# Routing and gathering of layer-one expert inputs as side steps of the context attention loop

## The reference

```python
x = x + _L1_xattn_ref(_layernorm(x), ctx_1024, ...)   # 8 heads of 64
x = x + _L1_ffn_ref(_layernorm(x), ...)
# _L1_ffn_ref, for each sequence:
logits = x @ router_w + router_b                      # 112 x 8
top_k_logits, expert_indices = jax.lax.top_k(logits, 2)
expert_probs = jax.nn.softmax(top_k_logits)
pos = cumsum(one_hot(first choices, then second)) ... - 1   # rank of a row within its expert
expert_inputs = buf.at[ei, pos].add(xr)               # 8 x 33 x 256, rows beyond 33 are dropped
# then silu((einp @ w_c_fc + b) * (einp @ w_gate + b)) @ w_c_proj + b, and each row collects its two outputs
```

## Time and profile before

| | |
|---|---|
| median of 3 runs | 1946.5 us (1944.9 to 1956.9) |
| profiled execution | 1952.7 us, its span 1951.1 us |
| mean granted TensorE clock | 0.946 |
| PE busy | 1719.9 us (88% of the span) |
| DVE busy | 1177.2 us (60%) |
| ACT busy | 828.2 us (42%) |
| POOL busy | 452.9 us (23%) |

### The profile page before, as it was taken

One profiled execution on the slowest core, in us unless ns is written; L12 is line 12 of the kernel. 1 busy time (PEld: TensorE's weight loads), 2 busy tenths in 40 slices (PEclk: granted clock), 3 DMA queues, 4 the chain that ended last, 5 costly groups with the idle time before them and its releaser, 6 DMA issues. The chain is left out here.

```text
span 1951.1 us, 39011 instructions
## 1 busy us (share of the span) xinstructions
PE 1719.9 (88%) x13070; PEld 1375.2 (70%) x13070; DVE 1177.2 (60%) x2667; ACT 828.2 (42%) x2420; POOL 452.9 (23%) x710
## 2 busy tenths in 40 slices
PE   3887689999998687799999949999999759999998
PEld 2555456666666476688888837777787649999996
DVE  3887546777777443366666534666665365666657
ACT  1332345555555123244444424444444245554534
POOL 1111201222222222212112021111111006544523
PEclk9999789999999699799999969999999879999999
DMA  8000133333350433000000000000000122312101
GB/s 241 0 0 0 55 93 125 119 123 123 123 171 11 151 119 120 20 11 13 11 9 12 4 24 24 17 16 16 21 10 1 40 90 70 126 66 93 37 1 38
DMA packets 87656, 114.20 MB, mean 59 GB/s; under 512 B 4832, under 2 KB 77071, under 8 KB 87311
## 3 DMA queue, kind: packets, MB, share of 16 engines
q1 hardware_dynamic: 82382, 99.91, 16.0%
q0 software_dynamic: 5184, 13.11, 2.0%
HBM read 65.04 MB, written 47.97 MB: 58 GB/s over the span
## 5 line engine op out<-in xcount | busy, mean ns | idle before, releaser
L1215 PE MATMUL ps<-e_ex_high,e_w_high 128*128 128x264 f32 x512 | 146.8, 287 | 5.4 <-POOL e_w_low L2475 5.4
L1215 PE MATMUL ps<-e_ex_high,e_w_low 128*128 128x264 f32 x512 | 146.5, 286 | 0.0
L1215 PE MATMUL ps<-e_ex_low,e_w_high 128*128 128x264 f32 x512 | 146.2, 286 | 0.0
L931 ACT ACTIVATE c_probs<-ps,c_negmax 112x375 f32<-112x375 f32 x256 | 143.7, 581 | 2.1 <-DVE c_negmax L1028 2.1
L1028 DVE TENSOR_REDUCE c_negmax<-ps 112x2 f32<-112x750 f32 x128 | 114.2, 934 | 34.7 <-PE ps L1152 34.7
L1814 PE MATMUL ps<-xnT,s_qkv 128*128 (+1 forms) x1024 | 130.5, 285 | 2.0 <-DVE xnT L1661 1.0
L1121 PEld LDWEIGHTS ps<-const,c_probs 112*125 112x125 f32 x768 | 99.0, 193 | 45.3 <-DVE c_pT L1044 19.4
L1814 PEld LDWEIGHTS ps<-xnT,s_qkv 128*128 128x128 f32 x1024 | 123.2, 199 | 6.4 <-DVE xnT L1661 1.7
L1628 ACT ACTIVATE s_probs<-ps,s_negmax 112x112 f32<-112x112 f32 x256 | 86.7, 365 | 74.8 <-DVE s_negmax L1677 74.8
L1121 PE MATMUL ps<-const,c_probs 112*125 112x112 f32 x768 | 115.1, 287 | 3.5 <-DVE c_pT L1044 2.0
L2004 ACT ACTIVATE c_probs<-ps,c_negmax 112x375 f32<-112x375 f32 x128 | 71.7, 574 | 83.1 <-DVE c_negmax L2060 83.1
(11 more groups left out here) (361 smaller groups left out, 4600.2 us busy)
## 6 DMA issues: line engine op xcount, KB each, us to landing
expert_rows<-d_zero SPq DMA_DIRECT2D x16, 2240.0 KB, 12.1
c_ctx_in<-in_ctx SPq DMA_DIRECT2D x32, 375.0 KB
e_wgt<-in_L_ffn_w_gate SPq DMA_DIRECT2D x8, 1024.0 KB, 5.0
e_wfc<-in_L_ffn_w_c_fc SPq DMA_DIRECT2D x8, 1024.0 KB, 7.2
e_wpj<-in_L_ffn_w_c_proj SPq DMA_DIRECT2D x8, 1024.0 KB, 9.6
e_x_in<-expert_rows SPq DMA_DIRECT2D x44, 128.0 KB, 2.0
expert_rows<-e_y POOLq DMA_DIRECT2D x44, 128.0 KB, 2.0
s_qkv<-in_L_attn_W_qkv SPq DMA_DIRECT2D x1, 3072.0 KB, 11.2
```

The costliest lines, as they stand in the source:

```text
L931: last = nc.scalar.activation(probs[:, g % 2, r, :], ps[:T, r, 0:S], ACT.Exp, bias=negmax[:, par, h:h + 1], accum_out=sums[:, par, h:h + 1])
L1215: last = nc.tensor.matmul(out, a, b, start=start and n == 0, stop=stop and n == len(pairs) - 1)
```

## The change

The first two parts of `experts_1` are gone. A class `Dispatch1` does their work sequence by sequence inside the loop of `context_attention_1`, as four more side steps: "logits" and "ranks" of sequence i - 2 on the bank that VectorE copies, "slots0" and "slots1" (the two halves of the columns) of sequence i - 3 on ScalarE's. The loop therefore runs to i = 18. VectorE takes the two best experts with its search for the maxima, reading PSUM (`take_best`), marks them (`mark_experts`), masks the ranks (`take_ranks`), finds the slots (`select_slots`) and builds the matrix of zeros and ones (`one_hot`), all in its own order between the steps of attention. The router's bias comes in as a third product. GpSimd keeps the two best logits. `rows_ready` writes the rows once. The rows' transposes go to a small tile `own` in place of `xnT`. The weights of expert 0 are loaded at the start of context attention, those of expert 1 at the start of the expert stage, and the softmax of the two best logits is taken there, ahead of the first rounding. To make room, large tiles of layer-one self attention lie in the weights of layer zero's experts, and some early loads come in another order. Slots are counted from 1. `BLOCKS` is 43.

```diff
-BLOCKS = 2 * ROWS // TILE + E0
+BLOCKS = (2 * ROWS - E0) // TILE + E0
...
+class Dispatch1:
...
+    def logits(self, pe, bank, q, u):
...
+        for c in range(2):
+            nc.tensor.matmul(bank[:T, 0:E1], self.own[:, u, c, :], self.w.router[:, c, :], start=(c == 0), stop=False)
+        return nc.tensor.matmul(bank[:T, 0:E1], self.sh.c("ones")[0:1, :T], self.w.router_b[0:1, :], start=False, stop=True)
+
+    def take_best(self, dve, bank, q, u):
...
+        self.link(dve, q, 1, nc.vector.max(self.best[:, u, :], bank[:T, 0:E1]))
+        return nc.vector.max_index(self.best_at[:, :], self.best[:, u, :], bank[:T, 0:E1])
+
+    def mark_experts(self, dve, q, taken):
...
+        self.link(dve, q, 2, nc.vector.tensor_copy(self.chosen[:, :], self.best_at[:, 0:2]))
+        nc.vector.tensor_tensor(self.sh.hot[:, q, :, :], mid(self.sh.c("expert_ids")[:T, 0:E1], 2), bc(self.chosen[:, :], E1),
+                                ALU.is_equal).then_inc(self.hot_ready, 1)
+
+    def rank_products(self, pe, bank, q):
...
+        pe.wait_ge(self.hot_ready, q + 1)
+        nc.tensor.matmul(bank[:T, 0:E1], self.sh.c("upto")[:T, :], self.sh.hot[:, q, 0, :], start=True, stop=True)
+        nc.tensor.matmul(bank[:T, E1:2 * E1], self.sh.c("upto")[:T, :], self.sh.hot[:, q, 1, :], start=True, stop=False)
+        return nc.tensor.matmul(bank[:T, E1:2 * E1], self.sh.c("ones")[:T, :], self.sh.hot[:, q, 0, :], start=False, stop=True)
...
+    def select_slots(self, dve, q, taken):
...
+        self.link(dve, q, 3, nc.vector.tensor_reduce(self.sh.slot[:, q, :], self.ranks[:, :, :], AX.X, ALU.add))
...
+        for k in range(2):
+            last = nc.vector.tensor_scalar(self.sel[:, k, :], self.sh.c("slots")[:T, :], self.sh.slot[:, q, k:k + 1], None, ALU.is_equal)
+        last.then_inc(self.sel_ready, 1)
...
+    def one_hot(self, eng, q):
...
+        for k in range(2):
+            on.tensor_tensor(self.part[:, k, :, :], bc(self.sh.hot[:, q, k, :], CAP), mid(self.sel[:, k, :], E1), ALU.mult).then_inc(self.part_ready, 1)
...
+        on.tensor_tensor(self.oneh[:, :, :], self.part[:, 0, :, :], self.part[:, 1, :, :], ALU.add).then_inc(self.oneh_ready, 1)
...
-    side = Side([("result", -1, ON_DVE), ("query", 1, ON_ACT), ("key0", 1, ON_DVE), ("context0", 2, ON_ACT),
-                 ("key1", 1, ON_DVE), ("key2", 1, ON_ACT),
-                 ("key3", 1, ON_DVE), ("value0", 1, ON_ACT), ("value1", 1, ON_DVE), ("context1", 2, ON_ACT),
+    side = Side([("result", -1, ON_DVE), ("query", 1, ON_ACT), ("slots0", -3, ON_ACT), ("key0", 1, ON_DVE), ("context0", 2, ON_ACT),
+                 ("slots1", -3, ON_ACT), ("key1", 1, ON_DVE), ("logits", -2, ON_DVE), ("key2", 1, ON_ACT),
+                 ("key3", 1, ON_DVE), ("value0", 1, ON_ACT), ("value1", 1, ON_DVE), ("ranks", -2, ON_DVE), ("context1", 2, ON_ACT),
...
+            load_expert(sh, sp, e1, 0, 0, e1.even)
...
                 evacuate("query", i, par)
+                evacuate("slots0", i, par)
                 copy_probs(i, 0, 1)
                 evacuate("context0", i, par)
+                evacuate("slots1", i, par)
                 copy_probs(i, 0, 3)
...
-                nc.vector.tensor_scalar(sh.XN[:, i - 1, :], x, ln.mv[:T, 0:1], ln.rstd[:T, :], ALU.subtract, ALU.mult)
...
                 evacuate("key1", i, par)
-                rows_ready(i)
+                evacuate("logits", i, par)
+                rows_ready(i, 1 - par)
                 maxima(i, 1)
+                if within(i - 2):
+                    dispatch.mark_experts(dve, i - 2, (side_done[ON_DVE], side.done("logits", i)))
...
                 copy_probs(i, 1, 2)
+                evacuate("ranks", i, par)
+                if within(i - 2):
+                    dispatch.select_slots(dve, i - 2, (side_done[ON_DVE], side.done("ranks", i)))
+                    dispatch.one_hot(dve, i - 2)
                 evacuate("rows", i, par)
                 evacuate("inverse", i, par)
...
                 aside("key0", i, par)
+                aside("slots0", i, par)
+                transposes(i, 0, 2)
                 aside("context0", i, par)
-                transposes(i, 0, 2)
                 aside("key1", i, par)
                 transposes(i, 0, 3)
+                aside("slots1", i, par)
+                aside("logits", i, par)
                 aside("key2", i, par)
...
                 transposes(i, 1, 2)
+                aside("ranks", i, par)
                 aside("context1", i, par)
...
-            sequences_ahead(pe, 3, iteration)
+            sequences_ahead(pe, 3, iteration, 2)
```

More of the change, by code:

```diff
@@ L1516, in within, with sequences_ahead, self_attention_1 @@
     return not isinstance(q, int) or 0 <= q < B
-def sequences_ahead(eng, ahead, iteration):
-    for i in range(-ahead, 1):
+def sequences_ahead(eng, ahead, iteration, behind=0):
+    start = 2 * behind + 1
+    for i in range(-ahead, start):
         iteration(i, i % 2)
-    with eng.Fori(1, B - 4, 2) as i:
+    with eng.Fori(start, B - 4, 2) as i:
         iteration(i, 1)
         iteration(i + 1, 0)
-    for i in range(B - 3, B + 1):
+    for i in range(B - 3, B + 1 + behind):
         iteration(i, i % 2)
-def self_attention_1(nc, sh, w):
+def self_attention_1(nc, sh, w, spare):
     H, DH, HALF = 16, 64, 4 * T
@@ L1930, in context_attention_1 @@
         side_done = [sem("side_done_act"), sem("side_done_dve")]
+        dispatch.slots_done = (side_done[ON_ACT], lambda i: side.done("slots1", i))
         block = ctx.enter_context(nc.Block())
@@ L2171, in aside @@
                     for c in range(2):
-                        last = nc.tensor.transpose(bank[:, c * T:(c + 1) * T], xn[:, c * 128:(c + 1) * 128], ident[:T, :T])
+                        last = nc.tensor.transpose(bank[:, c * T:(c + 1) * T], dispatch.xn[:, 1 - par, c * 128:(c + 1) * 128], ident[:T, :T])
+                elif name in ("slots0", "slots1"):
+                    last = dispatch.slot_products(pe, bank, i - 3, 1 - par, int(name[-1]))
+                elif name == "logits":
+                    last = dispatch.logits(pe, bank, i - 2, par)
+                elif name == "ranks":
+                    last = dispatch.rank_products(pe, bank, i - 2)
                 elif name == "query":
```

288 lines of the change are left out of this document (140 added, 148 removed).

## The result

| | before | after |
|---|---|---|
| median | 1949.38 us (1944.90 to 1956.92, 4 runs) | 2032.08 us (2026.72 to 2035.97, 4 runs) |
| profiled execution: span, mean clock | 1951.1 us, 0.946 | 2031.5 us, 0.934 |

The ratio is 1.0418, with a 95% interval of 1.0375 to 1.0462: slower, as forecast, but by some 80 us where 44 were forecast, and 22 us outside the range.

What follows compares the result with a forecast made beforehand. TensorE, in order and nearly full, was taken to bound the context attention loop. Terms -51.1 - 1.7 + 79 + 17.3 + 0.4 = +44 us on a median of 1946.5 gave 1990 us, range 1936 to 2010.

Steps and rivals of the forecast that it cites:

- What bounds the kernel: Layer-one context attention loop: TensorE alone sets the pace, busy 309.5 of 313 us, with a period of 22.7 us.
- Removed: Routing and gathering of expert inputs behind the loop: 51.1 us leave the path.
- tail of 17.3 + 0.4: Behind the attention: last sequences' side steps at half clock, 17.3 us; subtraction and exponential before the first rounding, 0.4.
- First half, +3.3: Loop iteration up to the value products: they start 3.3 us later, 1.33 work and the rest waits; bounds 1.3 to 4.
- Second half, +2.7: Loop iteration's ranks and one-hot chain on VectorE (2.24 us): inverse starts 2.7 us later; bounds 0.6 to 3.5.
- the sum left the loop at full clock: Loop of context attention: granted clock assumed to stay 1.00, as in the stretch from 100 to 150 us.
- rival 4: The clock falls inside the loop: at mean 0.9, 2.4 us more per iteration, 34 in all, 2024 us; chance 0.05.
- The sum: Whole kernel: -51.1 - 1.7 + 79 + 17.3 + 0.4 = +44 us, of which the loop is 79.
- 2.1 and 2.5: Last iteration with attention (i = 15): first half 2.1 us and second half 2.5 us later.
- Nothing later takes it back: Loop behind the value products: scores, maxima and exponentials keep their distances to TensorE, so the two shifts add up.
- One block fewer, 1.7: Layer zero's experts: one block fewer saves one period of that stage, 1.7 us.
- Hidden loads: Loads of experts 0 and 1 are covered by other work; 3 us allowed each if either cover is gone.

Runs made afterwards that it cites:

- x2_copies: Changed kernel with ScalarE copying the probabilities of heads 1 and 3 ahead of the slots' two evacuations: 2027.59 us, ratio to before 1.0375.
- x4_port: Changed kernel with GpSimd's second context subtraction of an iteration waiting until the one-hot sum is done: 2026.31 us, ratio to before 1.0355.
- x3_fill: Changed kernel plus 24 unread products on TensorE just ahead of the inverse transposes: 2062.90 us, ratio to before 1.0553.
- y2: Changed kernel plus 12 unread products on TensorE just ahead of the inverse transposes: 2027.38 us, ratio to before 1.0359.
- y3: Changed kernel with TensorE running the third value product ahead of the inverse transposes: 1995.53 us, ratio to before 1.0211.
- x1_behind: Changed kernel with VectorE's slot and one-hot chain moved behind its evacuations of rows and inverse: 1979.58 us, ratio to before 1.0109.
- z2: Kernel before, with GpSimd pausing before its fifth weight piece of every second expert in the expert stage: 1942.90 us, ratio to before 0.9948.
- y1_spread: Changed kernel with VectorE's chain split around its copies, probabilities copied ahead of slots, context's second half transposed ahead of ranks: 1968.26 us, ratio to before 1.0070.

## Why the prediction was right in sign and wrong in size

- **What bounds the kernel.** Right: TensorE's order in the loop decides, and the 51 us behind the loop are worth less than what they cost inside.
- **Removed.** 51.1 less the tail of 17.3 + 0.4 gives -33.4; measured from the last addition, -31.3. The tail is mostly at half clock, as forecast.
- **First half, +3.3.** Measured +2.9 (9.5 against 6.5). Of the three stalls, 1.38 stands for 1.4, 0.23 for 0.3 and nothing for 0.4: logits and bias keep TensorE busy for 0.95 us in that place (1415.82 to 1416.77), where the forecast had 0.6. x2_copies shows that part of the first stall is only moved when the copies change places.
- **Second half, +2.7.** The mechanism was right and the term too small: measured +3.8. The chain took 3.41 and not 2.24 us. 0.65 of the difference comes from GpSimd's subtraction beside the products (x4_port). Another 0.4 comes from the ranks times marks and their sum, for which I had no row: 0.25 each in the forecast, 0.44 measured, since VectorE stands 0.26 us before the step that reads the one ahead.
- **The step that failed: the sum left the loop at full clock.** That the clock falls inside the loop was rival 4, at 0.05, and outside the range. My argument against it was that the stretch from 100 to 150 us keeps 1.00 with TensorE busy only 42.5 of 50 us. A busy share over 50 us says nothing about one gap: the longest standstills in that stretch are of 1.0 us (`102.70 1.18 PE L344 MATMUL ps<-la_kvm,la_cqT 128*112 128x136 f32 x8 [1.00 <-DVE la_kvm L279]` in the trace before). In the loop after, TensorE is busy 41 to 45 of 50 us too, but stands still for 3.0 us once per iteration, and half clock follows each time. The trace before could have warned me: it has 18 standstills of TensorE of over 2 us, the kernel after 30, and behind each the clock is at its lower level for at least part of the next 3 us. Filling the standstill (x3, y2), shortening it with real work (y3) or removing it (x1) brings most of the clock back; shortening it to 2.4 (x4) does not. It costs 1.8 us per iteration; rival 4 had 2.4.
- **The sum.** With the measured terms, and 2.1 and 2.5 as forecast, 12 x 2.9 + 2.1 + 13 x (3.8 + 1.8) + 2.5 = 112 us against 113.5 measured and 79 forecast. 23 of the missing 34 us are the clock, 14 the longer chain, and the first half gives 5 back. The second half alone would have left the time inside the range: 1990 + 14 is 2004.
- **Nothing later takes it back.** Right in the changed kernel. In x1_behind something new comes later: 0.56 us at the result.
- **One block fewer, 1.7.** From the first block's load to the first context statistics both traces of the loop before (that of z2 too) have 475 us, the ten of the changed kernels 469 to 472: 4 us, though not from the block alone, since loads and addresses changed there too. The start of that stretch itself lies anywhere from 675 to 687 us, so most of the 10 us by which the first addition came early in this pair of traces is scatter.
- **Hidden loads.** Right: no wait for either expert's load shows. The context load that expert 0's now precede does come later: VectorE waits 1.7 us for it once at the start of the loop (at 1156.4 us), which it did not before; TensorE's first wait there is 12.5 us in place of 12.3.
- **Not in the forecast:** the long rounding, some 8 us when it happens.

## What to carry to other kernels

When a step moves into a loop whose period one engine sets, price it by the longest standstill that it causes, not only by its sum: here a wait of 3 us cost 3 us and then 1.8 more at half clock. Removing the long wait is not a full cure: y1_spread, with none, still loses the clock in five of eleven iterations. Put the part of a chain that nobody needs soon behind the copies that TensorE waits for: one chain moved behind two copies (x1_behind) gave back three quarters of the loss by the ratios, 1.0418 to 1.0109. And compute the room first: 51 us over 16 sequences, less a tail, are 2.3 us each, and the routing's products and hand-overs alone fill that.

## What the runs showed of the hardware

- After a standstill of TensorE of 3.0 or 2.4 us in an iteration that is otherwise nearly full, TensorE's clock is at its lower level (1.2 of 2.4 GHz) for part of what follows, in all nine iterations between 1250 and 1560 us of after, x2_copies and x4_port alike: some 6 us in the iteration shown (512-column products 0.43 us apart in place of 0.23), less in most. With 12 products of 64 columns in the gap it stays at the upper one in nine of ten iterations, with 24 in seven of nine.
- The clock also falls without such a standstill: in five of eleven iterations of y1_spread the longest one ahead of it is 0.4 us, and in two of x3_fill 0.6. No run here shows why, nor whether several short waits close together do it.
- VectorE's two products with both inputs in SBUF and GpSimd's subtraction hold each other up: 1.43 and 0.98 us together, 0.78 and 0.85 apart.
- A rounding on VectorE from SBUF to SBUF took 7.9 us, where 0.43 is the least, while GpSimd ran eleven instructions back to back, each at its usual length. The Trainium skill (SBUF — State Buffer, "SBUF: two separate sides") says that the shared pair of ports is a lock held for a whole instruction, by whoever starts first. The trace agrees that there is blocking, but if the lock is free after each instruction a rounding waits for one subtraction, 0.73 us, not for a row of them: here the measurement decides, and a row without a pause can shut VectorE out until it ends. It did so in 5 of the 9 traces of the changed expert stage without the pause, each time at the first rounding of the stage; in the other four no rounding took over 1.1 us. What makes the difference between the five and the four is not shown.
